# Attention on one Trainium2 core: the ten rounds of averages of a pair of heads, issued as five blocks of two rounds

## The chip, the cores and the metric

The kernel runs on one core of a Trainium2 chip. The metric is the device time of one execution in microseconds (us), here the median of several. The engines are named as in the profile: PE is the matrix engine (PEld its loads of the stationary operand), DVE the vector engine, ACT the scalar engine, POOL the general one, SP the engine that issues most transfers.

## The reference, cut to what matters

The program is two layers of a network; the change lies in the attention of the second one. With 4 sequences of 1024 tokens, 16 heads and 16 elements a head:

```python
Q, K = (apply_rope(Q), apply_rope(K))
scores = jnp.einsum('bhqd,bhkd->bhqk', Q, K) / jnp.sqrt(jnp.float32(d_k))
causal = jnp.tril(jnp.ones((S, S), dtype=bool))
scores = jnp.where(causal, scores, -jnp.inf)
attn = jax.nn.softmax(scores, axis=-1)
out = jnp.einsum('bhqk,bhkd->bhqd', attn, V)
```

## The kernel before

The program runs stage after stage on the one core: a scan layer, a layer of experts, the projection to queries and keys, then the function `attention`, its output projection, and a second layer of experts. Only `attention` is changed, which is about 560 us of the whole.

`attention` works on 32 pairs of heads (8 for each sequence) in 35 ticks. A tick has up to 18 steps, `i` from 0 to 17, and carries four pairs at once, each in another phase. On PE, whose order is written out by hand in the last loop of the function, a step holds in this order:

- chunk `i` (L1751) of pair `tick - 2`: 512 columns of transposed scores (keys by queries, maximum already subtracted through an extra row), into one of two buffers `t_ps_st`. ACT takes the exponential (L1707) and writes `t_probs`. Chunk `i` waits until the exponential `i - 2` is through, since it uses its buffer.
- at `i == 2`, one transpose of the row maxima (L1743) of pair `tick - 1`, negated on ACT (L1700).
- unit `i` (L1736), for `i` below 16, of pair `tick`: the scores of 128 queries against all the keys up to them, 128 to 1024 columns, into one of two buffers `t_ps_s`. DVE adds the mask `later` and takes the maximum of each row in one operation (L1690), followed by a short read of the accumulator. Unit `i` waits for DVE to be through with unit `i - 2`. In even pairs the widths are 1024, 128, 896, 256, 768, 384, 640, 512, 512, 640, 384, 768, 256, 896, 128, 1024; in odd pairs each two are swapped.
- rounds of averages (L1767) of pair `tick - 3`: each round is four matmuls, one for each strip of 32 columns of the array, which multiply 17 columns of values and ones (`t_vs`) with 256 columns of `t_probs` (128 in rounds 8 and 9) and add up in the one buffer `t_ps_o`. Each shows as two matmuls in the trace, so a round is eight. After round 9, ACT takes `t_ps_o` out (L1714), between the exponentials 16 and 17.

Which rounds stand behind which step is the table `avg_at`. The causal mask on the diagonals of `t_probs` is set by POOL (L1667). Where a round needs exponentials or masks, it waits for them; these are of the pair before, and nearly all are long done.

A chunk and a unit use the whole array, with 128 columns of weights; a round uses it in four strips with 17 columns each. I call the first kind full matmuls below.

Of the kernel before, what the change touches and what calls it, by code (L numbers as in the profile page):

```python
# [6 lines left out]
BF16 = mybir.dt.bfloat16  # L7
# [5 lines left out]
P = 128  # L13
# [1511 lines left out]
def attention(nc, sb, pb, sem, c, qkt_dram, v_dram, heads_dram):  # L1525
# [6 lines left out]
    NC = TPB  # L1532
# [8 lines left out]
    qs = sb("t_qs", [P, 2 * RINGQ, SEQ], FP32R)  # L1541
    v_raw = sb("t_v_raw", [P, NC, DM])
    vs = sb("t_vs", [P, 2, NC, NH, VR])
    later = sb("t_later", [P, NC * P])
    seen = sb("t_seen", [P, 2, NC * P], BF16)
    row_max = sb("t_row_max", [P, 2, 2 * NC])
    neg_max = sb("t_neg_max", [2 * NC, 2, P], FP32R)
# [37 lines left out]
    NR = len(lanes[0])  # L1585
    NU = len(units[0])
    NX = 2 * NST
    avg_at = {0: (0,), 2: (1,), 4: (2,), 6: (3,), 7: (4,), 9: (5,), 11: (6,), 13: (7,), 15: (8,), 16: (9,)}

    zeroed, q_zeroed, filled, set_up = sem("t_zeroed"), sem("t_q_zeroed"), sem("t_filled"), sem("t_set_up")  # L1590
    qk_loaded = [sem(f"t_qk_loaded{s}") for s in range(RINGQ)]
# [669 lines left out]
def build(nc, x, w_in, w_abc, w_out, norm_w, gate_w, gate_b, w1, b1, w2, b2, w_qkv, w_o, rope, w_route, w_gu, w_d,  # L2261
# [34 lines left out]
    with ExitStack() as whole:  # L2296
# [19 lines left out]
        with nc.Block() as block:  # L2316
            @block.gpsimd
            def _(pool):
                pool.sem_clear(range(min(used), max(used) + 1))

        phase(attention, c, qkt_dram, v_dram, headst_dram)
        wsb = lambda n, s, d=FP32: whole.enter_context(nc.sbuf_tensor(n, s, d))
        wgu_sb, wd_sb = wsb("wgu_sb", [P, KD, E1 * 2 * F1]), wsb("wd_sb", [P, F1 // P, E1 * DM])
# [70 lines left out]
```

## Time and profile before

| | |
|---|---|
| median of 3 runs | 1931.21 us (1927.43 to 1932.78) |
| profiled execution, its own time | 1926.69 us |
| its span in the profile | 1924.9 us |
| attention, first to last matmul of it, about | 942 to 1499 us of the span |
| mean granted clock of PE | 0.92 of full over the span |

The profiled execution is 4.5 us shorter than the median; what is worked out from its trace is added to either. Busy shares of PE say little, since matmuls are pipelined and their ends are modelled: how long PE takes is read from where the next instruction starts.

### The profile page before, as it was taken

What the parts mean: (1) busy time and instruction counts of PE and PEld (TensorE: products, weight loads), DVE (VectorE), ACT (ScalarE), POOL (GpSimd) and SP (SyncE); (2) the same over time, 40 slices, a digit from 0 to 9 for tenths busy, and PEclk for the clock granted to TensorE, in tenths of its full rate; (3) what the DMA queues carried; (4) which work ended last, traced back from release to release, by engine and by line L of the source; (5) the groups of instructions that cost most, each with busy time, mean ns of one, the idle gap of its engine ahead of it and who ended that gap; (6) DMA issues with size and microseconds to landing.
All of it is one profiled execution on the core that took longest, in us unless ns stands there. A gap on an engine that the chain in (4) does not pass through costs nothing. (4 is left out here: it accounts for less than half of the span.)

```text
span 1924.9 us, 28980 instructions
## 1 busy us (share of the span) xinstructions
PE 1601.7 (83%) x9337; PEld 1074.9 (56%) x9337; DVE 1022.4 (53%) x2851; ACT 705.2 (37%) x1457; POOL 565.6 (29%) x993
## 2 busy tenths in 40 slices
PE   1999999955999996885599999999999299869910
PEld 0577777643666664543355555555554178758810
DVE  1344544451222222786677777777773268855533
ACT  0444444411222221222056666666667011134400
POOL 2222443341000002784312322222323135500056
PEclk9899999977999998897799999999999689979965
DMA  8000111112121213685845655655650655445444
GB/s 303 27 22 30 51 53 45 45 66 82 63 67 63 66 58 117 186 284 193 141 57 80 102 78 81 105 84 85 98 81 26 176 186 158 146 145 157 149 133 148
DMA packets 151056, 204.02 MB, mean 106 GB/s; under 512 B 20608, under 2 KB 119424, under 8 KB 150656
## 3 DMA queue, kind: packets, MB, share of 16 engines
q1 hardware_dynamic: 104304, 131.12, 30.5%
q10 hardware_dynamic: 34320, 37.50, 5.7%
q0 software_dynamic: 12288, 33.57, 5.4%
q8 instruction: 80, 1.31, 0.3%
q14 instruction: 64, 0.52, 0.1%
HBM read 116.91 MB, written 84.93 MB: 105 GB/s over the span
## 5 line engine op out<-in xcount | busy, mean ns | idle before, releaser
L1690 DVE CUSTOM_DVE_ANT_0 t_seen<-t_ps_s,t_later 128x1024 bf16<-128x1024 f32 (+7 forms) x512 | 375.2, 757 | 148.8 <-PE t_ps_s L1736 145.9
L1707 ACT ACTIVATE t_probs<-t_ps_st 128x512 f32<-128x512 f32 x576 | 330.1, 597 | 189.9 <-PE t_ps_st L1751 185.4
L1751 PE MATMUL t_ps_st<-t_qs,t_ks 128*128 128x512 f32 (+3 forms) x768 | 262.3, 390 | 0.8 <-ACT t_probs L1707 0.5
L1667 POOL TENSOR_SCALAR_AFFINE_SELECT t_probs<-t_probs 128x128 f32<-128x128 f32 x512 | 139.5, 302 | 358.9 <-ACT t_probs L1707 357.7
L1736 PE MATMUL t_ps_s<-t_ks,t_qs 96*128 96x512 f32 (+3 forms) x768 | 239.8, 366 | 4.5 <-DVE t_row_max L1690 4.2
L1751 PEld LDWEIGHTS t_ps_st<-t_qs,t_ks 128*128 128x128 f32 x768 | 132.9, 190 | 136.6 <-ACT t_probs L1707 102.3
L1767 PE MATMUL t_ps_o<-t_probs,t_vs 128*17 128x256 f32 (+1 forms) x2560 | 185.0, 363 | 2.3 <-POOL t_probs L1667 1.8
L1349 POOL DMA_INDIRECT d_ye<-outputs_dram,r_pos_all x64 | 64.3, 1004 | 325.9 <-POOLq L1112 308.1
L1736 PEld LDWEIGHTS t_ps_s<-t_ks,t_qs 96*128 96x128 f32 x768 | 134.4, 191 | 34.7 <-DVE t_row_max L1690 23.6
L849 PE MATMUL ps_h<-w_in,xnt 128*128 128x512 f32 x256 | 125.4, 614 | 22.9 <-ACT xnt L683 22.9
L1144 PE MATMUL m_ps_h<-w_sb,m_xt 128*128 x284 | 135.4, 599 | 0.0
L1159 PE MATMUL m_ps_y<-w_sb,m_ht 128*128 x568 | 134.2, 379 | 0.0
L1187 DVE TENSOR_TENSOR m_h<-m_ps_h,b_sb 128x512 f32<-128x512 f32 x71 | 49.1, 691 | 128.7 <-PE m_ps_h L1144 128.7
L1214 ACT ACTIVATE m_xt<-m_ps_x 128x256 f32<-128x256 f32 x150 | 57.6, 384 | 158.8 <-PE m_ps_x L1137 158.7
L2237 POOL DMA_INDIRECT f_ye<-outputs_dram,r_pos_all x64 | 60.7, 949 | 172.7 <-PEq L2231 153.5
L1224 ACT ACTIVATE m_ht<-m_ps_ht 128x128 f32<-128x128 f32 (+1 forms) x150 | 63.9, 426 | 127.8 <-PE m_ps_ht L1152 127.8
L1159 PEld LDWEIGHTS m_ps_y<-w_sb,m_ht 128*128 128x128 f32 x568 | 102.5, 190 | 11.0
L1137 PE MATMUL m_ps_x<-ident,m_x_t 128*128 128x128 f32 x300 | 58.8, 279 | 48.9 <-DMA m_x_t<-gathered_dram 47.8
L355 POOL TENSOR_TENSOR xi<-xi,sig_z 128x512 f32<-128x512 f32 x32 | 40.7, 1271 | 160.2 <-ACT sig_z L695 160.1
L1767 PEld LDWEIGHTS t_ps_o<-t_probs,t_vs 128*17 128x17 f32 x2560 | 43.7, 95 | 76.7 <-ACT t_probs L1707 43.7
L1198 DVE TENSOR_TENSOR m_y<-m_ps_y,b_sb 128x256 f32<-128x256 f32 x71 | 30.1, 425 | 104.8 <-PE m_ps_y L1159 104.8
L1144 PE MATMUL m_ps_h<-wgu_sb,m_xt 128*128 x316 | 83.0, 386 | 0.0
(312 smaller groups left out, 2672.1 us busy)
## 6 DMA issues: line engine op xcount, KB each, us to landing
m_x_t<-gathered_dram SPq DMA_DIRECT2D x150, 128.0 KB, 2.0
outputs_dram<-m_y ACTq DMA_DIRECT2D x150, 128.0 KB, 1.7
t_qs<-qkt_dram SPq DMA_DIRECT2D x128, 128.0 KB, 5.5
t_ks<-qkt_dram SPq DMA_DIRECT2D x128, 128.0 KB, 5.8
qkt_dram<-d_hi SPq DMA_DIRECT2D x32, 256.0 KB, 4.1
qkt_dram<-d_lo SPq DMA_DIRECT2D x32, 256.0 KB, 4.1
headst_dram<-t_att SPq DMA_DIRECT2D x32, 256.0 KB, 7.5
x_t<-in_x_dram SPq DMA_DIRECT2D x8, 512.0 KB, 4.7
```

The lines of the kernel that those rows point to most:

```text
L849: last = nc.tensor.matmul(ps_h[h][:], xnt[:, n % 2, j, :], w_in[:, j, h * DI:(h + 1) * DI], start=(j == 0), stop=(j == KD - 1))
L1144: last = nc.tensor.matmul(ps_h[t % 2][:], xt[:, t % 2, j, :], w_up[:, j, bass.ts(expert[t], width)], start=(j == 0), stop=(j == KD - 1))
L1159: last = nc.tensor.matmul(ps_y[t % 2][:], ht[:, t % 2, j, :], w_down[:, j, bass.ts(expert[t], DM)], start=(j == 0), stop=(j == blocks - 1))
L1224: nc.scalar.activation(ht[:, t % 2], ps_ht[t % 2][:], ACT.Relu if relu else ACT.Copy).then_inc(ht_ready, 1)
L1349: nc.gpsimd.indirect_dma_start(out=ye[:, g % 2, j, i, :], out_offset=None, in_=outputs[:, :], in_offset=bass.IndirectOffsetOnAxis(ap=kept[ ...
L1667: nc.gpsimd.affine_select(out=diag, in_=diag, compare_op=ALU.is_ge, fill=0.0, base=0, pattern=[[1, P]], channel_multiplier=-1).then_inc(ma ...
L1690: nc.vector.tensor_tensor_reduce(out=seen[:, i % 2, 0:width], in0=ps_s[i % 2][:, 0:width], in1=later[:, NC * P - width:], scale=1.0, scala ...
L1707: nc.scalar.activation(probs[:, p % 2, i // NST, base:base + STC], ps_st[i % 2][:], ACT.Exp, scale=HD ** -0.5).then_inc(exp_ready, 1)
L1736: last = nc.tensor.matmul(ps_s[i % 2][:, k0:k1], qs[0:MAX_ROW, at, qc * P:(qc + 1) * P], ks[0:MAX_ROW, at, k0:k1], start=True, stop=True)
L1751: last = nc.tensor.matmul(ps_st[i % 2][:, col:col + width], ks[:, at, kc * P:(kc + 1) * P], qs[:, at, q0:q0 + width], start=True, stop=True)
L1767: last = nc.tensor.matmul(ps_o[32 * g:32 * g + VR, col:col + width], vs[:, (p // PAIRS) % 2, kc, 2 * (p % PAIRS) + head, :], probs[:, p % ...
L2237: nc.gpsimd.indirect_dma_start(out=ye[:, t % R, i, :], out_offset=None, in_=outputs[:, :], in_offset=bass.IndirectOffsetOnAxis(ap=kept["po ...
```

## The change

The table `avg_at` gives the steps behind which rounds are issued. It now has five entries of two rounds each in place of ten of one. The mask `later`, the second operand of the operation on DVE, is stored as bf16 in place of f32.

```diff
-    later = sb("t_later", [P, NC * P])
+    later = sb("t_later", [P, NC * P], BF16)
...
-    avg_at = {0: (0,), 2: (1,), 4: (2,), 6: (3,), 7: (4,), 9: (5,), 11: (6,), 13: (7,), 15: (8,), 16: (9,)}
+    avg_at = {1: (0, 1), 5: (2, 3), 8: (4, 5), 12: (6, 7), 16: (8, 9)}
```

The first place is PE's order in the tick of an even pair, from unit 1 (the first row) to unit 4. A row is one matmul as the program has it, with `x4` for four alike. Before:

```order
L1736 MATMUL t_ps_s<-t_ks,t_qs 128x128
L1751 MATMUL t_ps_st<-t_qs,t_ks 128x512
L1743 MATMUL t_ps_max<-ident,t_row_max 16x128
L1736 MATMUL t_ps_s<-t_ks,t_qs 128x512
L1736 MATMUL t_ps_s<-t_ks,t_qs 128x384
L1767 MATMUL t_ps_o<-t_probs,t_vs 17x256 x4
L1751 MATMUL t_ps_st<-t_qs,t_ks 128x512
L1736 MATMUL t_ps_s<-t_ks,t_qs 128x256
L1751 MATMUL t_ps_st<-t_qs,t_ks 128x512
L1736 MATMUL t_ps_s<-t_ks,t_qs 128x512
L1736 MATMUL t_ps_s<-t_ks,t_qs 128x256
```

The same place, from unit 1 to unit 4, of the changed kernel:

```order
L1736 MATMUL t_ps_s<-t_ks,t_qs 128x128
L1767 MATMUL t_ps_o<-t_probs,t_vs 17x256 x8
L1751 MATMUL t_ps_st<-t_qs,t_ks 128x512
L1743 MATMUL t_ps_max<-ident,t_row_max 16x128
L1736 MATMUL t_ps_s<-t_ks,t_qs 128x512
L1736 MATMUL t_ps_s<-t_ks,t_qs 128x384
L1751 MATMUL t_ps_st<-t_qs,t_ks 128x512
L1736 MATMUL t_ps_s<-t_ks,t_qs 128x256
L1751 MATMUL t_ps_st<-t_qs,t_ks 128x512
L1736 MATMUL t_ps_s<-t_ks,t_qs 128x512
L1736 MATMUL t_ps_s<-t_ks,t_qs 128x256
```

Two rounds now stand ahead of unit 2 (896 columns, the rows with 512 and 384), and none between unit 2 and unit 4.

The second place is the end of the same tick on PE, from unit 12 (the first row) to chunk 16. Before:

```order
L1736 MATMUL t_ps_s<-t_ks,t_qs 128x256
L1751 MATMUL t_ps_st<-t_qs,t_ks 128x512
L1736 MATMUL t_ps_s<-t_ks,t_qs 128x512
L1736 MATMUL t_ps_s<-t_ks,t_qs 128x384
L1767 MATMUL t_ps_o<-t_probs,t_vs 17x256 x4
L1751 MATMUL t_ps_st<-t_qs,t_ks 128x512
L1736 MATMUL t_ps_s<-t_ks,t_qs 128x128
L1751 MATMUL t_ps_st<-t_qs,t_ks 128x384
L1751 MATMUL t_ps_st<-t_qs,t_ks 128x128
L1736 MATMUL t_ps_s<-t_ks,t_qs 128x512 x2
L1767 MATMUL t_ps_o<-t_probs,t_vs 17x128 x4
L1751 MATMUL t_ps_st<-t_qs,t_ks 128x256 x2
```

The same place, from unit 12 to chunk 16, of the changed kernel:

```order
L1736 MATMUL t_ps_s<-t_ks,t_qs 128x256
L1767 MATMUL t_ps_o<-t_probs,t_vs 17x256 x8
L1751 MATMUL t_ps_st<-t_qs,t_ks 128x512
L1736 MATMUL t_ps_s<-t_ks,t_qs 128x512
L1736 MATMUL t_ps_s<-t_ks,t_qs 128x384
L1751 MATMUL t_ps_st<-t_qs,t_ks 128x512
L1736 MATMUL t_ps_s<-t_ks,t_qs 128x128
L1751 MATMUL t_ps_st<-t_qs,t_ks 128x384
L1751 MATMUL t_ps_st<-t_qs,t_ks 128x128
L1736 MATMUL t_ps_s<-t_ks,t_qs 128x512 x2
L1751 MATMUL t_ps_st<-t_qs,t_ks 128x256 x2
```

Rounds 6 and 7 now stand between unit 12 and unit 13, and nothing but chunks and a narrow unit between unit 13 (896 columns) and unit 15 (1024 columns, the row with `x2`).

## Rows read from the trace of the kernel before

**Rows 1.** Busy time by stretch, two ticks of attention. Columns: us, busy by engine.
```profile
core 0: us, PE busy (x) PEld busy (x) DVE busy (x) ACT busy (x) POOL busy (x), PEclk, DMA share, GB/s
1056.34:1089.36 33.02, 33.00 (x260) 18.08 (x259) 23.68 (x65) 21.61 (x41) 9.09 (x32) 1.00 0.69 113
```

**Rows 2.** Order of time on PE, at the two ends of those two ticks. Columns: start, us.
```profile
1056.34 0.27 PE L1743 MATMUL t_ps_max<-ident,t_row_max 128*16 128x128 f32 x1
...
1089.36 0.27 PE L1743 MATMUL t_ps_max<-ident,t_row_max 128*16 128x128 f32 x1
```

**Rows 3.** Waits, longest first, from 1050 to 1400 us: total, times, longest.
```profile
PEld t_ps_s L1736 <- DVE t_row_max L1690: 9.4, 41, 0.4
PEld t_ps_o L1767 <- POOL t_vs L1659: 2.2, 2, 1.5
```

**Rows 4.** Order of time from 1082.8 to 1086.7 us, unit 12 to chunk 16.
```profile
1082.88 0.28 PE L1736 MATMUL t_ps_s<-t_ks,t_qs 96*128 96x256 f32 x1
...
1083.01 0.40 PE L1751 MATMUL t_ps_st<-t_qs,t_ks 128*128 128x512 f32 x1
...
1083.24 0.58 PE L1736 MATMUL t_ps_s<-t_ks,t_qs 96*128 96x512 f32 x2
...
1083.75 0.63 PE L1767 MATMUL t_ps_o<-t_probs,t_vs 128*17 128x256 f32 x8
1083.86 1.09 DVE L1690 CUSTOM_DVE_ANT_0 t_seen<-t_ps_s,t_later 128x896 bf16<-128x896 f32 x1 [0.22 <-PE t_ps_s L1736]
...
1084.31 0.50 PE L1751 MATMUL t_ps_st<-t_qs,t_ks 128*128 128x512 f32 x1
...
1085.01 0.30 PEld L1736 LDWEIGHTS t_ps_s<-t_ks,t_qs 96*128 96x128 f32 x2
1085.01 0.72 PE L1736 MATMUL t_ps_s<-t_ks,t_qs 96*128 96x512 f32 x2
...
1086.01 0.50 PE L1751 MATMUL t_ps_st<-t_qs,t_ks 128*128 128x256 f32 x2
```

**Rows 5.** Order of time in the last two ticks: a short round, ten rounds together.
```profile
1488.17 1.09 ACT L1707 ACTIVATE t_probs<-t_ps_st 128x512 f32<-128x512 f32 x2 [0.39 <-PE t_ps_st L1751]
...
1492.41 0.41 PE L1767 MATMUL t_ps_o<-t_probs,t_vs 128*17 128x128 f32 x8
...
1494.48 4.08 PE L1767 MATMUL t_ps_o<-t_probs,t_vs 128*17 128x256 f32 x80 [0.45 <-issue]
```

**Rows 6.** Order of time from 1070.9 to 1076.8 us, units 1 to 5.
```profile
1072.45 0.23 PE L1736 MATMUL t_ps_s<-t_ks,t_qs 96*128 96x128 f32 x1
...
1073.78 1.09 DVE L1690 CUSTOM_DVE_ANT_0 t_seen<-t_ps_s,t_later 128x896 bf16<-128x896 f32 x1 [0.56 <-PE t_ps_s L1736]
...
1074.93 0.61 PE L1736 MATMUL t_ps_s<-t_ks,t_qs 96*128 96x512 f32 x2
...
1076.37 0.34 PE L1736 MATMUL t_ps_s<-t_ks,t_qs 96*128 96x384 f32 x1
```

**Rows 7.** Order of time on ACT: when the last ticks' averages are taken out.
```profile
1468.72 0.59 ACT L1714 ACTIVATE t_att<-t_ps_o 128x512 f32<-128x512 f32 x1
...
1481.38 0.59 ACT L1714 ACTIVATE t_att<-t_ps_o 128x512 f32<-128x512 f32 x1
...
1493.79 0.59 ACT L1714 ACTIVATE t_att<-t_ps_o 128x512 f32<-128x512 f32 x1
```

**Rows 8.** Groups on DVE by shape: count, busy us, mean ns, idle before.
```profile
L1690 DVE CUSTOM_DVE_ANT_0 t_seen<-t_ps_s,t_later 128x1024 bf16<-128x1024 f32 x64 | 78.4, 1225 | 59.4 <-PE t_ps_s L1736 59.4
...
L1187 DVE TENSOR_TENSOR m_h<-m_ps_h,b_sb 128x512 f32<-128x512 f32 x71 | 49.1, 691 | 128.7 <-PE m_ps_h L1144 128.7
L1690 DVE CUSTOM_DVE_ANT_0 t_seen<-t_ps_s,t_later 128x512 bf16<-128x512 f32 x64 | 44.1, 689 | 13.8 <-PE t_ps_s L1736 13.7
```

## The prediction

> **What bounds the kernel now.** Only attention changes, so I read that stretch alone. First the busy times of two ticks, an even and an odd one [rows 1]: 33.02 us, in which DVE is busy 23.7 and ACT 21.6. Neither is full, and PE's 33.0 is no measure, since its ends are modelled. So I read PE in order of time and ask at each instruction what it stood for. The waits [rows 3] show that PE's loads stood for DVE, but for 9.4 us only in 350 us. PE sets the pace, and it is nearly never held up.
>
> How PE spends its time shows in the rows around a round [rows 4]. Full matmuls of 512 columns start 0.23 us apart (1083.01, 1083.24) and end 0.40 after their start, so 0.23 is streaming and some 0.16 a tail. Unit 13 ends at 1083.82; the round begins at 1083.75, 0.07 before that end, and the next full matmul at 1084.31, 0.56 after the round. That full matmul takes 0.50, not 0.39 to 0.40: its weights weren't loaded ahead, 0.11. So around each round 0.09 is lost before it (0.16 of tail less 0.07), and 0.11 behind it, besides what it loses itself.
>
> What a round itself streams: alone, 256 columns take 0.63 [rows 4] and 128 take 0.41 [rows 5], so 128 more cost 0.22; a round of 256 streams 0.43, one of 128 some 0.21, and 0.20 is its tail. The last tick has the ten rounds in a row: 4.08 us [rows 5], and 8 x 0.43 + 2 x 0.21 + 0.20 gives 4.06. Rounds in a row follow each other without a gap.
>
> **What the change gives.** A second round in a block costs 0.43, not 0.56, and spares the 0.09 and the 0.11: 0.33 us for each of five in a tick, 1.65 us. There are 31 ticks with rounds among other work, so 51 us, if nothing else changed. Here a rule speaks for the change: the Trainium skill, TensorEngine Tiling (Array Packing), Key Properties, says that changing the tiling mode drains the engine. By this rule fewer changes are a gain; the trace agrees on the price (the 0.33), but the rule says nothing of who waits for PE meanwhile.
>
> **What the change takes.** There are two buffers `t_ps_s`, so unit i + 2 can't start before DVE is through with unit i. A wide unit takes DVE 0.96 to 1.23 us, while PE's own work up to the unit after next, two chunks and two units, streams about 1.0. A single round (0.76 with its losses) fills just what is missing. Two in one place (1.19) hold back the next unit and with it DVE, and where no round stands PE has nothing to fill DVE's time with. I walk this at two places. The rules are all from rows: a full matmul ends 0.455 ns a column after the one before (0.23 for 512); a block begins 0.07 before that end; the next load follows after 0.56 for one round, 0.99 for two; the full matmul behind ends 0.50 later; DVE starts 0.04 after the unit's end (1083.82, 1083.86); from its start to the load of the unit after next is 1.15 for 896 columns (1083.86 to 1085.01) [rows 4].
>
> Unit 12 to chunk 16 in an even tick, from the end of unit 12 as zero. Before, from rows: unit 13 ends at 0.66, its DVE starts at 0.70, unit 15 loads at 1.85 and ends at 2.57, a round, and chunk 16 ends at 3.35 [rows 4]. After: the block's two rounds begin at -0.07, chunk 13 loads at 0.92 and ends at 1.42, unit 13 (512 and 384 columns) ends at 1.82. DVE starts at 1.86, so unit 15 loads at 3.01. Chunk 14, unit 14 and chunk 15 are done at 2.6, so PE stands some 0.6 us. Unit 15 takes 0.72 as before, ends at 3.73, and chunk 16 at 3.96. That is 0.6 us longer; 0.22 of it is only that two full rounds (6 and 7) stand here where a full and a short one (7 and 8) stood, the rest is waiting, more than the change of mode spares.
>
> Unit 1 to unit 5 in an even tick: before, 1072.68 to 1076.71, 4.03 us [rows 6]. After: the block, chunk 2 ends at 1.42, the transpose 0.06 later, unit 2 at 1.94 (its first load takes 0.11, not 0.06), DVE starts at 1.98, unit 4 loads at 3.13, where PE has stood since about 2.2. It ends 0.61 later [rows 6], 3.74, chunk 5 and unit 5 add 0.40: 4.14. That is 0.1 longer, with the same number of rounds (the block of 0 and 1 here, 1 and 2 there).
>
> I stepped the same recurrence, with ACT's two buffers in it too, through both ticks and both orders. The old order gives 4.04, 3.07, 3.38, 3.34, 2.71 us in an even tick (unit 1 to 5, to 8, to 12, chunk 16, next unit 1) and 3.82, 3.13, 3.66, 3.05, 2.71 in an odd one, 32.91 together; the trace has 33.02 [rows 2]. The new order gives 4.16, 3.19, 3.60, 3.99, 2.71 and 4.10, 3.06, 4.00, 3.10, 2.30: 34.21. So two ticks lose 1.30 us: PE's work shrinks, but its waits grow from about 0.9 to 3.4 us a tick. Some of these are for ACT: round 0 stood between chunks 0 and 1, and chunk 1 needs the exponential of chunk 17, which now comes later than PE. 29 ticks hold chunks, units and rounds together: 14.5 x 1.30 = 18.9 us.
>
> Two ticks more have chunks and rounds but no units: 12.66 and 12.41 us now [rows 7]. There a chunk waits for the exponential of the chunk two before: 0.04 + 0.60 + 0.05 + 0.50 = 1.19 us from end to end, and the next one follows ACT's pace, 0.49 (two in 1.09 [rows 5]). A stretch of four steps with a block takes -0.07 + 0.99 + 0.50 + 1.19 + 0.49 = 3.10, one of three 2.61, the last, with the take-out on ACT, about 2.3: 3 x 3.10 + 2.61 + 2.3 = 14.2. That is 1.5 to 1.8 more in each, 3.2 us together.
>
> **The rest.** At two joins of batches round 0 waited 2.2 us for the values [rows 3]; it now stands one step later and gives back up to 1 us. No transfer moves on its queue: SP's loads hang on chunks and on the maxima, as before. The other rounds move forward or back by one step, and their exponentials and masks are of the pair before, so no new wait for POOL. The last tick is ten rounds in a row in both.
>
> **The mask in bf16.** No row has this operation with a bf16 mask. At 512 columns it takes 689 ns, an f32 addition of a PSUM and an SBUF operand 691 [rows 8]; from 512 to 1024 columns it grows by 1.05 ns an element. One operand, the scores in PSUM, stays f32, and I take the price as unchanged. The bounds are a rate twice as high (512 columns less 0.27 us) and a few per cent more. The Trainium skill, VectorE: DVE Perf Modes, Why PSUM operands drop a tier, has any f32 PSUM operand at one element a cycle; by it too the sum stays as it is, and no run here shows it yet.
>
> **The sum.** 18.9 + 3.2 - 0.5 = 21.6, about 22 us. Against the profiled execution's own 1926.7 that is 1948.7; it ran 4.5 us under the median, so against the median 1931.2 + 22 = 1953.
>
> **The rivals.** (a) Fewer changes of mode win: the waits don't grow, because the operations between hide them, and the 51 us come: 1880. For it speaks that PE is nearly never held up now [rows 3]; against it both walks, in which the wait follows from two buffers. It needs the new waits to stay under 2.5 us a tick; I find 3.4. (b) The bf16 mask makes DVE faster, and this pays for the block. My recurrence breaks even at a DVE that is about a fifth faster, and gives 22 us less than before, 1909, at 0.6 of its time. Against it stand the f32 operand and the equal 689 and 691 ns [rows 8]. (c) Rounds of a block don't follow without a gap, so a second one costs 0.56 with its drain: 5 x 0.13 x 31 = 20 us more, 1973. The 4.08 us of ten rounds speak against it [rows 5]. (d) The loss is there, but PE's loads, pulled ahead, or ACT's earlier start eat most of it: within 6 us of 1931. The recurrence leaves room for 0.1 us in two ticks, not for 1.3.
>
> **How the numbers follow.** The forecast, slower by 14 to 31 us, 0.80; (c) or another larger loss 0.06; (a) 0.03; (b) 0.04; (d) 0.07. With the latencies of the recurrence doubled, or DVE's and ACT's operations 5% longer in both orders, the difference stays at 20 to 25 us; a mask that costs DVE 2% either way moves it by 3, and three runs of a median by another 3. So the range is 1943 to 1963. A measurement of this kernel tells about 0.3%, 6 us, from no change. Faster by more 0.06, within 0.07, slower by more 0.87.
>
> **What would show it.** In the profile after: blocks of `x16` on L1767, the next full matmul 0.99 us after the block's start; two ticks of transposes 34.2 to 34.4 us apart, the longer one about 17.7; idle of L1736's loads on DVE several times 9.4 us; the take-outs of the last ticks about 14.2 us apart; DVE's 1024 columns at 1225 ns. The forecast is wrong if these columns get cheaper by a tenth or more, if the waits for DVE don't grow, or if a block takes 1.1 us.

## The result and the profile after

The changed kernel takes 1945.63 us (median of 4 runs, 1943.57 to 1945.92), the kernel before 1929.89 (median of 4, 1927.43 to 1932.78): a ratio of 1.0079, 95% interval 1.0061 to 1.0096. It is 15.7 us slower, 11.8 to 18.5 by the interval; 22 were forecast. The time lies in the forecast's 1943 to 1963 us, near the lower end.

The profiled execution took 1945.9 us, its span 1944.1. The stretch from the first unit to the last round shows where the time went. The view is that of a tile's instructions. Each line gives the count, the shortest, median and longest time in ns, and the starts of the first and the last. Before, from 942.5 to 1498.3, 555.8 us:

```profile
L1736 PE MATMUL t_ps_s<-t_ks,t_qs x768: 220/388/988, 942.5 to 1467.1; 96*128 96x512 f32 x80, 96*128 96x384 f32 x48, 96*128 96x256 f32 x48, 96*128 96x128 f32 x16
L1767 PE MATMUL t_ps_o<-t_probs,t_vs x2560: 272/379/393, 988.7 to 1498.3; 128*17 128x256 f32 x158, 128*17 128x128 f32 x39
```

After:

```profile
L1736 PE MATMUL t_ps_s<-t_ks,t_qs x768: 220/390/988, 945.1 to 1483.9; 96*128 96x512 f32 x80, 96*128 96x384 f32 x48, 96*128 96x256 f32 x48, 96*128 96x128 f32 x16
L1767 PE MATMUL t_ps_o<-t_probs,t_vs x2560: 272/379/393, 990.9 to 1518.0; 128*17 128x256 f32 x158, 128*17 128x128 f32 x39
```

That is 572.9 us, 17.1 more. The two profiled executions differ by 19.2 us in all; attention also starts 2.6 us later (945.1 against 942.5), and nothing is changed ahead of it.

Two ticks, an even and an odd one, by the same view as [rows 1]:

```profile
1060.69:1094.95 34.26, 32.18 (x260) 18.85 (x259) 23.35 (x66) 21.58 (x40) 10.24 (x38) 1.00 0.68 108
```

34.26 us in place of 33.02, with PE's clock at full rate in both; DVE and ACT do what they did before. PE's modelled busy time fell by 0.8 us while the ticks grew by 1.2. The waits from 1050 to 1400 us, as in [rows 3], name who took the rest:

```profile
PEld t_ps_st L1751 <- ACT t_probs L1707: 39.2, 113, 0.7
PEld t_ps_s L1736 <- DVE t_row_max L1690: 35.7, 71, 0.8
...
PE t_ps_s L1736 <- DVE t_row_max L1690: 15.7, 41, 0.5
...
PE t_ps_st L1751 <- ACT t_probs L1707: 4.2, 10, 0.4
```

The loads of units stand 35.7 us for DVE, 9.4 before; PE itself is now listed as waiting for DVE too, 15.7 us, which it was not in this stretch before. And the wait of round 0 for values at the joins of batches [rows 3] is gone.

The end of an even tick, unit 12 to chunk 16, in order of time, as in [rows 4]:

```profile
1086.70 0.28 PE L1736 MATMUL t_ps_s<-t_ks,t_qs 96*128 96x256 f32 x1
...
1086.91 1.06 PE L1767 MATMUL t_ps_o<-t_probs,t_vs 128*17 128x256 f32 x16
...
1087.89 0.50 PE L1751 MATMUL t_ps_st<-t_qs,t_ks 128*128 128x512 f32 x1
...
1088.23 0.57 PE L1736 MATMUL t_ps_s<-t_ks,t_qs 96*128 96x512 f32 x2
...
1088.84 1.09 DVE L1690 CUSTOM_DVE_ANT_0 t_seen<-t_ps_s,t_later 128x896 bf16<-128x896 f32 x1 [0.86 <-PE t_ps_s L1736]
...
1089.99 0.30 PEld L1736 LDWEIGHTS t_ps_s<-t_ks,t_qs 96*128 96x128 f32 x2 [0.61 <-DVE t_row_max L1690]
1089.99 0.74 PE L1736 MATMUL t_ps_s<-t_ks,t_qs 96*128 96x512 f32 x2 [0.41 <-DVE t_row_max L1690]
...
1090.57 0.40 PE L1751 MATMUL t_ps_st<-t_qs,t_ks 128*128 128x256 f32 x2
```

Read it from the end of unit 12, at 1086.98. The block of sixteen matmuls takes 0.98 us up to the next full one (1087.89 less 1086.91), where two single rounds would take twice 0.56. DVE has nothing for 0.86 us. Its operation on 896 columns then starts at 1088.84, and the next wide unit stands for it until 1089.99. Chunk 16 ends at 1090.97, 3.99 us after unit 12; before it was 3.35.

The other place of the change, units 1, 4 and 5 of the same tick, in order of time on PE:

```profile
1075.79 0.22 PE L1736 MATMUL t_ps_s<-t_ks,t_qs 96*128 96x128 f32 x1
...
1079.15 0.61 PE L1736 MATMUL t_ps_s<-t_ks,t_qs 96*128 96x512 f32 x2 [0.53 <-DVE t_row_max L1690]
...
1079.84 0.33 PE L1736 MATMUL t_ps_s<-t_ks,t_qs 96*128 96x384 f32 x1
```

From the end of unit 1 (1076.01) to that of unit 5 (1080.17) are 4.16 us, where 4.03 stood [rows 6]; unit 4 stands 0.53 us for DVE.

Of the two rows that bear on the mask, one has the operation on DVE, the other the plain addition beside it, as in [rows 8]:

```profile
L1690 DVE CUSTOM_DVE_ANT_0 t_seen<-t_ps_s,t_later 128x1024 bf16<-128x1024 f32 x64 | 78.4, 1225 | 50.0 <-PE t_ps_s L1736 50.0
...
L1187 DVE TENSOR_TENSOR m_h<-m_ps_h,b_sb 128x512 f32<-128x512 f32 x71 | 49.1, 692 | 129.8 <-PE m_ps_h L1144 129.8
```

1225 ns as before: the bf16 mask costs the same. The last ticks, by when ACT takes the averages out, as in [rows 7], and the ten rounds of the last one:

```profile
1485.21 0.60 ACT L1714 ACTIVATE t_att<-t_ps_o 128x512 f32<-128x512 f32 x1
...
1499.36 0.60 ACT L1714 ACTIVATE t_att<-t_ps_o 128x512 f32<-128x512 f32 x1
...
1513.53 0.60 ACT L1714 ACTIVATE t_att<-t_ps_o 128x512 f32<-128x512 f32 x1
```

14.15 and 14.17 us, where 12.66 and 12.41 stood.

### The profile page after: what moved, and what is told of

It is laid out like the page before. It is cut to its first block and busy times, and to the rows that moved or that the text cites. A ratio compares the mean times of both kernels' runs of the same rounds, so it can differ in the third digit from the quotient of the medians.

```text
span 1944.1 us, 28980 instructions
## 1 busy us (share of the span) xinstructions
PE 1585.5 (82%) x9337; PEld 1086.3 (56%) x9337; DVE 1018.3 (52%) x2851; ACT 704.4 (36%) x1457; POOL 563.7 (29%) x993
## 5 line engine op out<-in xcount | busy, mean ns | idle before, releaser
L1690 DVE CUSTOM_DVE_ANT_0 t_seen<-t_ps_s,t_later 128x1024 bf16<-128x1024 f32 (+7 forms) x512 | 371.1, 756 | 167.4 <-PE t_ps_s L1736 167.1
L1767 PE MATMUL t_ps_o<-t_probs,t_vs 128*17 128x256 f32 (+1 forms) x2560 | 154.9, 361 | 0.3 <-issue 0.3
L1767 PEld LDWEIGHTS t_ps_o<-t_probs,t_vs 128*17 128x17 f32 x2560 | 59.0, 96 | 62.3 <-issue 20.6
```

Source lines behind the costliest of these rows:

```text
L1690: nc.vector.tensor_tensor_reduce(out=seen[:, i % 2, 0:width], in0=ps_s[i % 2][:, 0:width], in1=later[:, NC * P - width:], scale=1.0, scala ...
L1767: last = nc.tensor.matmul(ps_o[32 * g:32 * g + VR, col:col + width], vs[:, (p // PAIRS) % 2, kc, 2 * (p % PAIRS) + head, :], probs[:, p % ...
```

## The experiments

The theory on trial is that of place: what a block of two rounds costs or gives depends on who waits behind it. Its first rival is that the mask has a part in the loss, its second that two rounds in one piece cost more than two single ones wherever they stand. All ten kernels are the kernel before with the edit shown. Times are medians beside the kernel before on the same chip; ratios are to that.

**One part of the change alone: the mask.**

```diff
-    later = sb("t_later", [P, NC * P])
+    later = sb("t_later", [P, NC * P], BF16)
```

> The old table of rounds, with only the mask stored as bf16. My theory (the mask costs DVE the same, and the loss comes from where the rounds stand): no change, within 3 us of the kernel before, the operation on 1024 columns at 1225 ns. The rival (the bf16 mask makes DVE's operation dearer or cheaper, and part of the 16 us is its doing): a difference of more than 6 us either way, with the 1024-column operation off 1225 ns by more than 2 per cent.

Measured: 1929.49 us against 1930.12, ratio 0.9991 (0.9982 to 1.0001). The operation on 1024 columns takes 1225 ns.

```profile
L1690 DVE CUSTOM_DVE_ANT_0 t_seen<-t_ps_s,t_later 128x1024 bf16<-128x1024 f32 x64 | 78.4, 1225 | 59.9 <-PE t_ps_s L1736 59.9
```

**The other part alone: the table, with the mask in f32.**

```diff
-    avg_at = {0: (0,), 2: (1,), 4: (2,), 6: (3,), 7: (4,), 9: (5,), 11: (6,), 13: (7,), 15: (8,), 16: (9,)}
+    avg_at = {1: (0, 1), 5: (2, 3), 8: (4, 5), 12: (6, 7), 16: (8, 9)}
```

> The new table of rounds with the mask left in f32. My theory: all of the loss is the order's, 14 to 20 us slower than the kernel before (median of the changed kernel: 15.7), two ticks at 34.25 us. The rival, that the mask takes a part: under 12 us.

Measured: 1947.51 against 1930.12, ratio 1.0094 (1.0078 to 1.0109), 17.4 us slower. Attention runs from 942.2 to 1515.2 us of the span in its trace, 573.0, as in the changed kernel. The mask has no part; the whole loss is the table's.

**One block, at the end of the tick.** The old table, but for rounds 8 and 9:

```diff
-    avg_at = {0: (0,), 2: (1,), 4: (2,), 6: (3,), 7: (4,), 9: (5,), 11: (6,), 13: (7,), 15: (8,), 16: (9,)}
+    avg_at = {0: (0,), 2: (1,), 4: (2,), 6: (3,), 7: (4,), 9: (5,), 11: (6,), 13: (7,), 16: (8, 9)}
```

> The old table, but rounds 8 and 9 together behind chunk 16, where no unit follows until the next tick. Theory of place (a block costs what the engines behind it must wait, and here nobody waits): the change of mode saved stays a gain, two ticks go from 33.02 to about 32.1 us, the kernel is 10 to 14 us faster. Rival (any block of two rounds costs time, since it is longer in one piece): as slow as or slower than before, by up to 4 us.

Measured: 1921.35 against 1930.12, ratio 0.9958 (0.9944 to 0.9972), 8.8 us faster: less than I expected, but of the sign. The transposes of the maxima, in order of time on PE, two ticks apart:

```profile
1102.52 0.27 PE L1743 MATMUL t_ps_max<-ident,t_row_max 128*16 128x128 f32 x1
...
1134.73 0.27 PE L1743 MATMUL t_ps_max<-ident,t_row_max 128*16 128x128 f32 x1
```

32.21 us, 0.8 less than 33.02 [rows 2]. At this rate 29 ticks give 11.7 us. In the trace attention is 10.6 us shorter (941.8 to 1487.0). A part was lost at the joins of batches, where the rounds now stand 4.0 us for the copies of the values and 3.2 for masks, 2.2 and 1.8 before; that the medians have only 8.8 lies within their interval (5.4 to 10.8 us).

**One block, in the midst of the wide units.** The old table, but rounds 6 and 7 stand together where the changed kernel has them:

```diff
-    avg_at = {0: (0,), 2: (1,), 4: (2,), 6: (3,), 7: (4,), 9: (5,), 11: (6,), 13: (7,), 15: (8,), 16: (9,)}
+    avg_at = {0: (0,), 2: (1,), 4: (2,), 6: (3,), 7: (4,), 9: (5,), 12: (6, 7), 15: (8,), 16: (9,)}
```

> The old table, but rounds 6 and 7 together behind unit 12, as in the changed kernel; the other eight stay single. Theory of place: this one block makes most of the loss, because the wide unit 13 (or 14) comes late and nothing fills the time until it is reduced: two ticks about 33.9 us, 12 to 18 us slower than before, with a wait for DVE of about 0.6 us in each tick. Rival (the loss is shared evenly by five blocks): 2 to 5 us slower.

Measured: 1944.58 against 1930.12, ratio 1.0081 (1.0068 to 1.0095), 14.5 us slower. Two ticks take 34.02 us:

```profile
1107.79 0.27 PE L1743 MATMUL t_ps_max<-ident,t_row_max 128*16 128x128 f32 x1
...
1141.81 0.27 PE L1743 MATMUL t_ps_max<-ident,t_row_max 128*16 128x128 f32 x1
```

One block spares one change of mode in both of these kernels. Behind chunk 16 it gives 8.8 us, behind unit 12 it takes 14.5. That falls on the side of place and leaves nothing of the second rival.

The loss isn't the same as the changed kernel's, though. Here the tick of an even pair (1124.95 less 1107.79) takes 17.16 us, some 0.6 more than before, and that of an odd pair 16.86, some 0.4 more. In the changed kernel the two are 1.1 and 0.1 longer. So the other four blocks take 0.5 us in one kind of tick and give back 0.3 in the other; only their sum is small, 34.26 against 34.02.

**Five blocks of the same pairs, elsewhere.**

```diff
-    avg_at = {0: (0,), 2: (1,), 4: (2,), 6: (3,), 7: (4,), 9: (5,), 11: (6,), 13: (7,), 15: (8,), 16: (9,)}
+    avg_at = {0: (0, 1), 2: (2, 3), 4: (4, 5), 13: (6, 7), 16: (8, 9)}
```

> Five blocks of the same pairs of rounds, but behind other steps: 0, 2, 4, 13 and 16 in place of 1, 5, 8, 12 and 16. As many changes of mode as in the changed kernel. Theory of place: the steps decide, so two ticks take about 32.6 to 32.7 us (the changed kernel 34.25, the kernel before 33.02), and the kernel is 0 to 8 us faster than before. Rival (blocks of two rounds are what costs): 12 us or more slower, as the changed kernel.

Measured: 1928.85 against 1929.62, ratio 0.9997 (0.9982 to 1.0012): no difference from the kernel before. The ratio is 0.97% under that of the new table alone (1.0094), with the same number of blocks. Two ticks take 32.63 us, as expected:

```profile
1105.32 0.27 PE L1743 MATMUL t_ps_max<-ident,t_row_max 128*16 128x128 f32 x1
...
1137.95 0.27 PE L1743 MATMUL t_ps_max<-ident,t_row_max 128*16 128x128 f32 x1
```

Its gain of 0.4 in two ticks is eaten elsewhere: in its trace attention takes 559.2 us (943.4 to 1502.6), 3.4 more than before. One place is the joins of batches, since rounds 0 and 1 stand at the very start of a tick: PE stands 3.6 us for the values and 2.9 for masks. The other is the ticks without units, by ACT's take-outs:

```profile
1481.69 0.60 ACT L1714 ACTIVATE t_att<-t_ps_o 128x512 f32<-128x512 f32 x1 [0.42 <-PE t_ps_o L1767]
...
1498.08 0.60 ACT L1714 ACTIVATE t_att<-t_ps_o 128x512 f32<-128x512 f32 x1
```

They take 15.74 (from 1465.95) and 16.39 us, where 12.66 and 12.41 stood: 7 us more in two ticks.

**Two blocks, where the recurrence finds them best.** I stepped the recurrence of the prediction through many tables and took one of the shortest:

```diff
-    avg_at = {0: (0,), 2: (1,), 4: (2,), 6: (3,), 7: (4,), 9: (5,), 11: (6,), 13: (7,), 15: (8,), 16: (9,)}
+    avg_at = {0: (0,), 2: (1, 2), 4: (3,), 6: (4,), 9: (5,), 11: (6,), 13: (7,), 16: (8, 9)}
```

> Eight places: round 0 behind step 0, rounds 1 and 2 behind 2, then 3 to 7 single behind 4, 6, 9, 11, 13, rounds 8 and 9 behind 16. Theory of place: two changes of mode fewer where nobody waits longer for it: two ticks 31.8 to 31.9 us, 11 to 16 us faster than before, and faster than with the last pair alone (8.8 us). Rival (the gain of the last pair is special to the steps without units, a block elsewhere costs): slower than with the last pair alone.

Measured: 1914.04 against 1929.62, ratio 0.9924 (0.9906 to 0.9941), 15.6 us faster; two ticks take 31.95 us (transposes at 1103.24 and 1135.19), a little over the 31.8 to 31.9 expected. The second block gives 0.13 us a tick over the run with the last pair alone, with rounds 3 and 4 moved as well.

**DVE's work taken away, with the old and the new table.** The operation on DVE now covers 128 columns whatever the unit's width, so the maximum of a row is taken over the last 128 keys alone. PE computes all the scores as before. The edit in both:

```diff
-nc.vector.tensor_tensor_reduce(out=seen[:, i % 2, 0:width], in0=ps_s[i % 2][:, 0:width],
-                               in1=later[:, NC * P - width:], scale=1.0, scalar=-3.0e38, op0=ALU.add,
+nc.vector.tensor_tensor_reduce(out=seen[:, i % 2, 0:P], in0=ps_s[i % 2][:, width - P:width],
+                               in1=later[:, NC * P - P:], scale=1.0, scalar=-3.0e38, op0=ALU.add,
```

With the old table:

> The old table, with DVE's operation cut to 128 columns: the maximum of a row is taken over the last 128 of its keys alone. Takes away what PE waits for on DVE. Two ticks about 32.1 to 32.2 us, 20 to 28 us faster than the kernel before; what is left of waiting is for ACT.

With the new table:

> The new table with DVE's operation cut to 128 columns, as in the run beside it. If the wait for DVE is what eats the gain of fewer changes of mode, the sign turns: 8 to 13 us faster than the old table with the same cut (two ticks about 31.1 to 31.3 us). Rival (the block is dear for another reason, its own length or the exponentials alone): the new table stays slower than the old one with the cut, by 10 us or more.

Measured: the old table 1911.80 (ratio 0.990, 0.988 to 0.9919), the new table 1896.98 (0.9828, 0.9811 to 0.9844), both against 1929.62. The new table is now 14.8 us faster than the old one, where with the full operation it is 15.7 to 17.4 slower. The old table's gain is 17.8, a little under the 20 to 28 expected; the difference between the two a little over the 8 to 13 (in attention's stretch of the traces it is 12.2: 535.1 and 522.9 us). About half of the old table's gain isn't from rounds at all: the first unit to the third transpose, which holds no rounds but the first one or two, takes 37.1 us in place of 47.8. The waits of the new table with the cut, from 1050 to 1400 us:

```profile
DVE t_seen L1690 <- PE t_ps_s L1736: 242.0, 322, 3.8
...
PEld t_ps_st L1751 <- ACT t_probs L1707: 45.7, 143, 0.7
```

No row of PE waiting for DVE is left in either kernel. Two ticks take 32.28 us in the old order and 31.17 in the new one (transposes at 1107.38 and 1138.55). This is the experiment that takes the disputed wait away and leaves the rest, and the sign turns. But 1.11 us in two ticks is a third of the 3.3 that ten spared changes of mode were priced at.

**POOL's loop turned round, with the old table and with the two blocks.** The joins had cost more in each better table. In the tick that starts a batch, POOL waits some 13 us for the transfer of the values, and the masks of the older pair stand behind it in its order. The edit lets them go first:

```diff
             for tick in range(pairs + 2):
-                if live(tick) and tick % PAIRS == 0:
-                    values(tick // PAIRS)
                 if live(tick - 2):
                     mask(tick - 2)
+                if live(tick) and tick % PAIRS == 0:
+                    values(tick // PAIRS)
```

With the two blocks:

> The table of the run with two pairs, and POOL's loop turned round: in the tick that starts a batch of 8 pairs, the masks of the older pair are made before POOL waits for the values of the batch and copies them. Theory: at the joins the rounds stood for masks and copies queued behind POOL's wait for a transfer (the ticks of 17.8 and 17.0 to 17.2 us); in the other order these ticks take as long as the rest, which gives 1 to 4 us more than the two pairs alone, 14 to 18 us faster than the kernel before. Rival: the waits move elsewhere in the tick and nothing changes.

With the old table:

> The old table with POOL's loop turned round, as in the run beside it. Theory: the two long ticks at the joins go, 1 to 3 us faster than the kernel before, at the edge of what can be told. Rival: no change, or slower if the copies now come late for round 0 of the new batch.

Measured: with two blocks 1913.15 against 1929.09, ratio 0.9917 (0.9902 to 0.9933), 15.9 us faster, the lowest ratio here among kernels that compute all of the result. The 1 to 4 us expected over the two blocks alone (0.9924) don't show in the medians; in the traces attention is 2.5 us shorter (537.6 against 540.1). With the old table 1927.31, ratio 0.9991 (0.998 to 1.0002), which a measurement can't tell from none. The traces can: the join whose tick took 17.9 us before (1204.90 to 1222.82) takes 16.55 in the old table with POOL turned round:

```profile
1206.90 0.27 PE L1743 MATMUL t_ps_max<-ident,t_row_max 128*16 128x128 f32 x1
...
1223.45 0.27 PE L1743 MATMUL t_ps_max<-ident,t_row_max 128*16 128x128 f32 x1
```

and no row of a round waiting for POOL is left in either. Attention is 1.8 us shorter for it in the old table (944.5 to 1498.5).

## Why the prediction was right, point by point

**The bound.** Right: PE sets the pace, in lockstep with DVE through two buffers. The cut of DVE's operation, which leaves PE's work as it was, took away all of PE's waits for DVE and turned the sign.

**The gain of fewer changes of mode.** The price is right: a block of two takes 0.98 us to the next full matmul (0.99 forecast), against twice 0.56. What it gives depends on the place too. Behind chunk 16 one block gave 0.8 us in two ticks, 0.40 in one, against 0.33 worked out; the second block of the two-block table gave 0.13. With DVE's work cut, five blocks gave 0.55 in a tick, against 1.65. So the 51 us were a bound that no kernel here came near. The rest of the gain was expected to go into waits for ACT, whose two buffers the recurrence has in it: it had the two ticks at 31.1 to 31.3 us, and they take 31.17. No run takes ACT's work away, so that this is ACT isn't shown.

The Trainium skill, TensorEngine Tiling (Array Packing), Key Properties, has a change of mode drain the engine. By that alone fewer blocks would be faster: the traces agree that a change has a price, and on the outcome for the table with the last pair (8.8 us faster), the one with two blocks (15.6), and the new one with DVE's work cut (14.8), but not for the changed kernel.

**The loss.** The first walk forecast the end of unit 13 at 1.82 us after unit 12, the start of DVE at 1.86, the load of unit 15 at 3.01 and the end of chunk 16 at 3.96. The trace has 1.82, 1.86, 3.01 and 3.99. One reading in it doesn't fit its own numbers: from 2.6, where PE was done, to 3.01 are 0.4 us of standing, not 0.6, and the trace has 0.41 on PE (0.61 on its loads). The second walk forecast 4.14, the trace has 4.16, with unit 4 at 3.14 (3.13 forecast). For the two ticks 34.21 was forecast and 34.26 measured; the transposes after lie at 1060.68, 1077.27 and 1094.94, so the ticks take 16.6 and 17.7 us, and the longer was forecast at about 17.7. The waits that the prediction put at 0.9 and 3.4 us a tick don't quite follow: 0.9, the 1.65 spared and the 0.65 lost make 3.2. The run with the block behind unit 12 alone loses 14.5 us, as much as nearly the whole, though spread otherwise over the ticks.

**The sum was too high.** 22 us were forecast; the medians differ by 15.7, attention's stretch of the two traces by 17.1. By the traces' transposes of the maxima, that stretch has three parts:

- From the third transpose to the last, 29 times from one to the next: 480.4 us before (990.25 to 1470.68) and 495.9 after (992.23 to 1488.11), 15.5 more, where 18.9 - 0.5 = 18.4 was forecast. The recurrence's 1.30 in two ticks is 1.24 in the traces (34.26 less 33.02), 18.0 in 29 ticks. Only 14 of these stretches are of the kind that loses 1.1 us, and 15 of the kind that loses 0.1, which takes off another 0.5. The joins were sized too small: round 0 one step later, and ticks that are longer, gave back the 1.4 and 0.6 us by which the two join ticks (17.92 and 17.14) stood over the others, 2.0, not the 0.5 taken.
- From the last transpose to the end: 2.3 us more. The take-outs of the ticks without units have 3.25 more (1.49 and 1.76), as the 3.2 forecast. But the first of them is counted from the take-out ahead of the last transpose, by 1.96 us before and 2.90 after; these 0.9 us stood in the 29 ticks already, and the sum had them twice.
- From the first unit to the third transpose: 0.6 us less (47.75 and 47.13), where nothing was forecast. The stretch from the second to the third transpose differs between traces of the same table: 17.01 us in the kernel before (973.24 to 990.25) and 16.18 in the run with the mask alone (973.87 to 990.05). What sets it I haven't tried.

Together 15.5 + 2.3 - 0.6 gives the 17.1 measured, within rounding. The mechanism held; the terms that were mis-sized are the joins and the 0.9 us counted twice, and each made the forecast too high.

**The mask.** Right: 1225 ns in either type, and no time by itself. The Trainium skill, VectorE: DVE Perf Modes, Why PSUM operands drop a tier, caps an f32 operand in PSUM at the lowest rate, so a narrower mask would give nothing; the equal 1225 ns agree.

**The rivals.** (a) Fewer changes of mode win: false of this table, true of others (8.8 and 15.6 us) and of this one when DVE's work is cut, though never by the 51 us. (b) The mask pays: false. (c) A gap between the rounds of a block: false, 0.98 us. (d) The loss is eaten to within 6 us: false, 15.7.

## What to carry to other kernels

When two instructions of one engine are put together to save a change of mode, ask first which buffers turn round in that time: with two buffers, the other engine's operation is on the path wherever it outlasts the work that stands between. The gain came only where no one waited longer for the block. Walk the order by hand with a few prices from the trace, for the widest case; here that gave each stretch of a tick to a few hundredths of a microsecond, and a better table too. And look at what stands behind a long wait in an engine's order: POOL's masks behind a transfer were cheap to move, though what it gave, some 2 us in the traces, is less than these times can tell.

## What the hardware showed that was not expected

The rows that say a load waited 0.4 us for ACT (68.9 us in all from 1050 to 1400 us before, at most 0.4 each) are hardly waits for ACT. In the stretch of [rows 4] the load at 1084.31 stands right behind a round, and the exponential that its chunk needs had ended some 0.6 us earlier: I read it as the gap of the change of mode. In the run with DVE's work cut they stay at 65.3 us in the old order, and fall to 45.7 in the new one, which has half the changes. That isn't proof: in the new order the rows that name no one behind such a load grow from 20.5 to 28.8 us, and single waits reach 0.7, so some are real there. A wait that is always of one length, behind one kind of instruction, is likely a cost of that instruction.

Place decides more than number: one block behind unit 12 costs 14.5 us alone, and one behind chunk 16 gives 8.8. The prediction's recurrence had already put more than half of an even tick's loss (0.65 of 1.11 us) behind unit 12.
